# Four edge buffers become six in the message passing of a graph network, and 124 edge groups become 122

## The reference

```
h = relu(layernorm(x));  L0: weighted means over edges, half of the features src->dst, half dst->src
h = relu(layernorm(x));  L1: graph convolution (segment sum of h[src] over dst), then top-2 of 64
                         expert MLPs (256-512-256, gelu) for each node, then batch norm
h = relu(layernorm(x));  L2 ("agnn"), 4 layers:
    logit = beta * cos(h[src], h[dst]);  m = segment_max(logit, dst)
    ex = exp(logit - m[dst]);            h = relu(segment_sum(ex * h[src]) / segment_sum(ex))
h = relu(layernorm(x));  L3 ("gat"), 3 layers, 4 heads of 64, self loops for nodes below 1250:
    h = x @ W;  e = leaky_relu(s_src[src] + s_dst[dst]);  softmax over the edges of a dst
    out = segment_sum(alpha * h[src], dst) + b
```

## Time and profile before

| | us |
|---|---|
| median of 3 runs | 9924.49 (9922.85 to 9927.99) |
| the profiled execution | 9927.93 |
| its span, first to last instruction | 9926.2 |

### The profile page before, as it was taken

The page is one execution under the profiler, slowest core; times in us unless marked ns, Lnnn a source line. Parts: engine busy times, 40 slices in busy tenths (PEclk is TensorE's granted clock), DMA queues, the critical chain, the costliest instruction groups (busy, mean ns, idle before and its releaser), DMA issues. The chain is left out here.

```text
span 9926.2 us, 160244 instructions
## 1 busy us (share of the span) xinstructions
PE 7005.6 (71%) x34788; PEld 5407.3 (54%) x34789; DVE 5926.7 (60%) x21625; ACT 2633.9 (27%) x6946; POOL 5383.8 (54%) x5578
## 2 busy tenths in 40 slices
PE   0003545535663982996996996996799989998997
PEld 0003445534442872885885885885466556655664
DVE  6003334442213225887887887887687768777777
ACT  0001100000000221222222222222455555555554
POOL 0675777747731112775775775774355445534553
PEclk9997557767775996998998998998677677776776
DMA  1301114453440991445445445444333323333333
GB/s 76 137 2 43 48 42 101 101 68 105 105 52 23 345 315 52 100 99 83 100 98 83 100 99 83 100 99 62 74 78 77 66 76 78 78 59 84 77 77 64
DMA packets 621385, 896.33 MB, mean 90 GB/s; under 512 B 289911, under 2 KB 427383, under 8 KB 620062
## 3 DMA queue, kind: packets, MB, share of 16 engines
q0 software_dynamic: 244928, 618.96, 28.9%
q1 hardware_dynamic: 376414, 276.94, 9.2%
HBM read 767.30 MB, written 135.40 MB: 91 GB/s over the span
## 5 line engine op out<-in xcount | busy, mean ns | idle before, releaser
L1510 POOL DMA_INDIRECT hs<-tab_agnn,rec x1984 | 1964.8, 990 | 1114.8 <-issue 593.9
L1944 POOL DMA_INDIRECT hs<-tab_gat,rec x1488 | 1406.4, 945 | 1282.6 <-DVE msg L2013 868.1
L2120 PE MATMUL psV<-msg,ohf 128*128 128x260 f32 x2976 | 1270.9, 603 | 0.8 <-DVE msg L2013 0.8
L1982 DVE CUSTOM_DVE_ANT_0 cand<-psL,neg 128x512 f32<-128x512 f32 x1488 | 991.5, 685 | 265.4 <-issue 176.4
L1531 DVE CUSTOM_DVE_ANT_0 prod<-psG,hs 128x256 f32<-128x256 f32 x1984 | 842.3, 480 | 421.1 <-DMA hs<-tab_agnn,rec 342.8
L2120 PEld LDWEIGHTS psV<-msg,ohf 128*128 128x128 f32 x2976 | 901.0, 317 | 204.1 <-issue 1.2
L1660 PE MATMUL psV<-hs,pr 128*128 128x258 f32 x3968 | 986.1, 392 | 6.2 <-DVE pr L1570 6.2
L1636 PE MATMUL psG<-HN,ohT 128*128 x3968 | 955.6, 384 | 5.1 <-ACT neg L1605 5.1
L626 PE MATMUL psT<-ident,oh 128*128 128x128 f32 x496 | 126.7, 405 | 1023.6 <-DVE oh L592 1023.6
L1636 PEld LDWEIGHTS psG<-HN,ohT 128*128 128x128 f32 x3968 | 725.6, 193 | 86.7 <-issue 6.1
L1660 PEld LDWEIGHTS psV<-hs,pr 128*128 128x128 f32 x3968 | 715.8, 190 | 89.5 <-DVE acc L1557 7.8
(11 more groups left out here) (326 smaller groups left out, 13438.2 us busy)
## 6 DMA issues: line engine op xcount, KB each, us to landing
w<-in_L_gnn_w SPq DMA_DIRECT2D x224, 512.0 KB, 6.0
fwd_d<-acc SPq DMA_DIRECT2D x10, 3224.0 KB, 44.2
fw<-fwd_d SPq DMA_DIRECT2D x124, 260.0 KB
hs<-tab_agnn,rec POOLq DMA_INDIRECT x1984
hs<-tab_gat,rec POOLq DMA_INDIRECT x1488
rec<-rec_d SPq DMA_DIRECT2D x1240, 8.0 KB, 1.7
b<-in_L_gnn_b SPq DMA_DIRECT2D x113, 128.0 KB, 6.4
x<-xbuf SPq DMA_DIRECT2D x112, 128.0 KB, 6.0
```

The lines of the kernel that those rows point to most:

```text
L1510: nc.gpsimd.indirect_dma_start(out=hs[:, j, g, :], out_offset=None, in_=k.tab_agnn, in_offset=bass.IndirectOffsetOnAxis(ap=rec[:, j, g, 0: ...
L1944: nc.gpsimd.indirect_dma_start(out=hs[:, j, g, :], out_offset=None, in_=k.tab_gat, in_offset=bass.IndirectOffsetOnAxis(ap=rec[:, j, g, 0:1 ...
L1982: V.tensor_tensor_reduce(cand[:, m, :], psL[:, m, :], neg[:, h2, :], 1.0, -BIG, ALU.add, ALU.max, mt[:, h2, m:m + 1]).then_inc(s_lt, 1)
L2120: mm = nc.tensor.matmul(psV[:, h4, 0:W_GAT], ohf[:, h4, g, :], msg[:, h4, g, :], start=(g == 0), stop=(g == G - 1))
```

## The change

The ring `U` is 6 in all nine passes, so `rec`, `hs`, `oh` and others get six slots, and a gather of group t waits for group t - 6. The experts keep a ring of 4 under the name `UE`. `NG` is no longer rounded up, so there are 122 groups; since 122 is not a multiple of 6, `pipeline` writes the last two groups out behind the loop, before the drain. The loop runs 19 times instead of 30, and its body is half as long again. Counts of semaphores by slot (`use`, `uses`) follow. In the scatter, fake edges get a place beyond the end of `rec_d`, and the DMA drops what is out of bounds (`bounds_check`). `rec_d` and `fwd_d` have 62,464 rows instead of 63,488.

```diff
@@ -25,10 +25,8 @@
-U = 4
+U = 6
 NG = (E + NB * (GE - 1)) // GE
-NG += -NG % U
-NI = NG // U
...
-MT += -MT % U
+UE = 4
+MT += -MT % UE
...
+def uses(j):
+
+    return NG // U + (j < NG % U)
...
-def pipeline(eng, step, drain, total=NG, numbers=None):
-
-
+def pipeline(eng, step, drain, total=NG, numbers=None, ring=U):
+
+
+    whole = total // ring
     if numbers:
         numbers.load(0)
-    for j in range(U):
+    for j in range(ring):
         step(0, j)
-    with eng.Fori(1, total // U) as i:
+    with eng.Fori(1, whole) as i:
         if numbers:
             numbers.load(i)
-        for j in range(U):
+        for j in range(ring):
             step(i, j)
-    if numbers and drain:
-        numbers.load(total // U)
-    for j in range(drain):
-        step(total // U, j)
+    for n in range(total % ring + drain):
+        if numbers and n % ring == 0:
+            numbers.load(whole + n // ring)
+        step(whole + n // ring, n % ring)
...
-                c.done(nc.vector.scalar_tensor_tensor(out=pos[:, 1, :], in0=mask[:, NB, 1, :], scalar=float(SPARE),
-                                                      in1=pos[:, 1, :], op0=ALU.mult, op1=ALU.add))
-                c.mark(nc.vector.tensor_copy(R[:, :, 4], pos[:, 0, :]))
-                c.mark(nc.vector.tensor_scalar(R[:, :, 3], pos[:, 1, :], float(SPARE), None, ALU.min))
+                c.done(nc.vector.scalar_tensor_tensor(out=pos[:, :, :], in0=mask[:, NB, :, :], scalar=float(SPARE),
+                                                      in1=pos[:, :, :], op0=ALU.mult, op1=ALU.add))
+                for n, col in ((0, 4), (1, 3)):
+                    c.mark(nc.vector.tensor_scalar(R[:, :, col], pos[:, n, :], float(SPARE), None, ALU.min))
...
                                 out=k.rec_rows, out_offset=bass.IndirectOffsetOnAxis(ap=slot[:, n, g, 4:5], axis=0),
-                                in_=slot[:, n, g, 0:4], in_offset=None).then_inc(s_sent[n], 16)
+                                in_=slot[:, n, g, 0:4], in_offset=None, bounds_check=SPARE - 1,
+                                oob_is_err=False).then_inc(s_sent[n], 16)
...
-        use = lambda i: turn * NI + i
+        use = lambda i, j: turn * uses(j) + i
```

More of the change, by code:

```diff
@@ L107, in pick, with lagged @@
     return tile[(slice(None), ds(i, 1)) + rest]
-def lagged(i, j, lag, total=NG):
+def uses(j):
+    return NG // U + (j < NG % U)
+def lagged(i, j, lag, total=NG, ring=U):
     j2 = j - lag
@@ L114, in lagged @@
     while j2 < 0:
-        i2, j2 = i2 - 1, j2 + U
-    t = i2 * U + j2
+        i2, j2 = i2 - 1, j2 + ring
+    t = i2 * ring + j2
     if isinstance(t, int) and not 0 <= t < total:
@@ L142, with __init__ @@
 class Numbers:
-    def __init__(self, nc, eng, table, name, top=NB - 1):
-        self.eng, self.table, self.top = eng, table, top
-        self.regs = [eng.alloc_register(tagged(nc, f"{name}{n}_")) for n in range(2 * U)]
+    def __init__(self, nc, eng, table, name, top=NB - 1, ring=U):
+        self.eng, self.table, self.top, self.ring = eng, table, top, ring
+        self.regs = [eng.alloc_register(tagged(nc, f"{name}{n}_")) for n in range(2 * ring)]
     def load(self, i):
-        self.eng.load(self.regs, self.table[:, ds(i * U, 2 * U)])
+        self.eng.load(self.regs, self.table[:, ds(i * self.ring, 2 * self.ring)])
     def at(self, j, lag):
-        return self.eng.snap(self.regs[U + j - lag], min_val=0, max_val=self.top)
+        return self.eng.snap(self.regs[self.ring + j - lag], min_val=0, max_val=self.top)
     def free(self):
@@ L467, in step @@
                     if not (isinstance(i, int) and i == 0):
-                        sp.wait_ge(q.gather[j], use(i) * (16 * G))
+                        sp.wait_ge(q.gather[j], use(i, j) * (16 * G))
                         sp.sem_inc(q.gate_sp, 1)
@@ L520, in step @@
                         pe.wait_ge(q.u, nth(t - 1))
-                    pe.wait_ge(q.gather[j], use(i) * (16 * G) + 16 * G)
+                    pe.wait_ge(q.gather[j], use(i, j) * (16 * G) + 16 * G)
                     for g in range(G):
@@ L557, in step @@
                     t = i * U + j
[L558 to L562, removed]
+                    if not (isinstance(i, int) and i == 0):
+                        sp.wait_ge(s_sent[j], i * (16 * G))
+                        sp.sem_inc(s_gate_sp, 1)
+                    sp.dma_start(rec[:, j, :, :], k.rec_d[:, ds(t * G, G), :]).then_inc(s_rec[j], 16)
                 pipeline(sp, step, 0)
@@ L1158, in experts @@
         s_b1c = sem("s_b1c")
-        s_x = [sem(f"s_x{n}") for n in range(U)]
-        s_w = [sem(f"s_w{n}") for n in range(U)]
+        s_x = [sem(f"s_x{n}") for n in range(UE)]
+        s_w = [sem(f"s_w{n}") for n in range(UE)]
         s_bias = sem("s_bias")
@@ L1167, in experts @@
         s_ys = sem("s_ys")
-        s_out = [sem(f"s_out{n}") for n in range(U)]
+        s_out = [sem(f"s_out{n}") for n in range(UE)]
         s_gate = sem("s_gate")
@@ L1217, in step @@
                 def step(i, n):
-                    t = i * U + n
+                    t = i * UE + n
                     pool.wait_ge(s_ys, t + 1)
@@ L1221, in step @@
                     pool.dma_start(k.ybuf_t[ds(t, 1), :, :].rearrange("a p c -> (a p) c"), y[:, n, :]).then_inc(s_out[n], 16)
-                pipeline(pool, step, 0, MT)
-                for n in range(U):
-                    pool.wait_ge(s_out[n], MT // U * 16)
+                pipeline(pool, step, 0, MT, ring=UE)
+                for n in range(UE):
+                    pool.wait_ge(s_out[n], MT // UE * 16)
             @block.vector
@@ L1250, in step @@
                         nc.vector.tensor_tensor(y[:, m, :], psy[:, m % 2, 0:D], b2[:, m, :], ALU.add).then_inc(s_ys, 1)
-                pipeline(dve, step, 2, MT, numbers=tiles)
+                pipeline(dve, step, 2, MT, tiles, UE)
             @block.scalar
@@ L1255, in step @@
                 def step(i, n):
-                    if last := lagged(i, n, 1, MT):
+                    if last := lagged(i, n, 1, MT, UE):
                         _, m, t = last
@@ L1265, in step @@
                         g.then_inc(s_g, 1)
-                pipeline(act, step, 1, MT)
+                pipeline(act, step, 1, MT, ring=UE)
             @block.tensor
@@ L1276, in step @@
                 def step(i, n):
-                    if now := lagged(i, n, 0, MT):
+                    if now := lagged(i, n, 0, MT, UE):
                         i0, m, t = now
@@ L1303, in step @@
                         mm.then_inc(s_y, 1)
-                pipeline(pe, step, 2, MT)
+                pipeline(pe, step, 2, MT, ring=UE)
 def combine(nc, k, a):
@@ L1485, in attention_by_angle @@
                 nth = lambda t: layer * NG + (2 * NG + t)
-                use = lambda i: layer * NI + (2 * NI + i)
+                use = lambda i, j: layer * uses(j) + (2 * uses(j) + i)
                 own = flow = lambda t: layer * NG + t
```

68 lines of the change are left out of this document (34 added, 34 removed).

## The result

| | us |
|---|---|
| kernel before | 9923.67 (9918.89 to 9927.99, 4 runs) |
| changed kernel | 9754.11 (9748.81 to 9756.55, 4 runs) |
| ratio, 95% interval | 0.9829 (0.9812 to 0.9846) |
| profiled execution of the change, its span | 9754.8, 9753.1 |

The change is faster by 170 us, or 1.7%. The forecast was 9656, a gain of 269; the time lies in the range of 9510 to 9790, near its slow end.

The account below looks back on a forecast made before the run. POOL, PE and DVE lie close in agnn's groups with edges, DMA bounds those without, PE bounds gat; -133 - 80 - 35 - 28 + 2 + 5 = -269 from 9927.9, less 3.4, gives 9656 (range 9511 to 9790).

Parts of the forecast that it names:

- loads of twelve numbers: Block-number loads in gat's loop: twelve instead of eight cost 0 to 0.30 us more each, 0 to 18 us, taken as 4.
- Two groups fewer: Every pass loses two groups without edges, at the price of its tail: 133 us saved together, called the surest term.
- No ring helps there: agnn's groups without edges: all gathers read one table row, DMA bounds them at 6.67 us; only fewer groups help.
- still at some 6.7 us: Sign for the profile after: agnn's groups without edges keep this pace, queue over 90% busy, but 11 of them.
- The ring in agnn: agnn's groups with edges: POOL's waits should vanish, pace from 5.43 to 5.25 us a group, 80 us saved (0 to 155).
- under 5 us a pass: Sign for the profile after: POOL's wait for PE's sums in agnn's groups with edges, before 28.6 us a pass.
- The ring in gat: gat's groups with edges: PE's 11.8 us a pass of waits for gathers go, 35 us saved (0 to twice that).
- rival 2: gat wins more, as six slots remove many slow groups: 133 us gained there instead of 63, time 9586; chance 0.13.
- fewer branches: gat's loop: 11 fewer branches a pass at 0.98 us, 32 us over three passes, net 28 after longer loads.
- Longer code: agnn's branches back between passes might start to pay a stall, 0 to 10 us, taken as 5; inner loops no refetch.
- rival 3: gat's loop no longer fits the code DVE holds; branches back cost up to 3.40 us each, at most +194, 9850; chance 0.07.
- Rivals 1 and 4: 1: POOL falls into step with DVE, ring wins nothing, 9798, chance 0.14; 4: gat's clock falls, slower, 10,025, chance 0.06.

Follow-up runs that it names:

- ring of 4: The changed kernel with a ring of 4 instead of 6, still 122 groups: 9800.40 us, 0.9876 of the kernel before; on a slower chip 0.9912.
- aligned: The changed kernel with each iteration's twelve block numbers stored apart, at multiples of 48 bytes: 9579.01 us, 0.9647 of the kernel before; on a slower chip 10,945.72, 0.9939.
- the body of 407: DVE's gat loop with a ring of 8 instead of 6, on the aligned kernel with pads spread over the table: 9624.95 us, 0.9697 of the kernel before.
- its repeat: The changed kernel run once more, unaltered, beside the second ring-of-4 run: 9758.71 us, 0.9829 of the kernel before.

## Why the prediction was right or wrong

The sign and the range held; the sum was 97 us too good. Two errors are behind that, and they go against each other: the loads of twelve numbers cost 176 us more than forecast, and the ring with short loads won 74 more. That the time fell within the range is in part luck.

| term | predicted | measured |
|---|---|---|
| two groups, scatter, outer code | -133 + 2 + 5 = -126 | -131 (ring of 4 against before) |
| ring and branches, loads of 12 aligned | -80 - 35 - 32 = -147 | -221 (aligned against ring of 4) |
| loads of 12 against 8 | +4 | +180 (change against aligned) |
| sum | -269 | -172 |

Where the time went shows by PE's sums, from the profiled executions: from the first group of a pass to its 111th, the last with edges, and from there to the last group, in us over the four passes of agnn and the three of gat.

| | before | ring of 4, 122 groups | change | aligned |
|---|---|---|---|---|
| agnn, to the 111th group | 2410 | 2397 | 2383 | 2300 |
| agnn, behind it | 330 | 287 | 254 | 257 |
| gat, to the 111th group | 2352 | 2340 | 2354 | 2253 |
| gat, behind it | 275 | 229 | 210 | 206 |

So the change won 27 us in agnn's groups with edges, where 80 were forecast, and lost 2 in gat's, where 63 were; the tails gave 141 instead of 97. The rows for agnn's first pass, of the ring of 4 and then of the aligned kernel, in each the sums of the first, the 111th and the last group:

```profile
3913.30 1.99 PE L1665 MATMUL psV<-hs,pr 128*128 128x258 f32 x8
4512.65 1.99 PE L1665 MATMUL psV<-hs,pr 128*128 128x258 f32 x8
4582.54 2.01 PE L1665 MATMUL psV<-hs,pr 128*128 128x258 f32 x8 [1.47 <-DVE pr L1575]
...
3934.40 1.99 PE L1670 MATMUL psV<-hs,pr 128*128 128x258 f32 x8
4509.07 1.99 PE L1670 MATMUL psV<-hs,pr 128*128 128x258 f32 x8
4572.60 2.01 PE L1670 MATMUL psV<-hs,pr 128*128 128x258 f32 x8 [1.47 <-DVE pr L1580]
```

*Two groups fewer.* Right in size; the 131 hold the longer outer code and the scatter, too.

*"No ring helps there."* This step of the prediction failed, to the change's good. From the ring of 4 to the aligned ring of 6 the groups without edges took 30 us less in agnn and 23 in gat, though the queue was still 93% busy. The sign that I gave for it, "still at some 6.7 us", failed with it: it was 5.6.

*The loads of twelve numbers.* This is the step that cost the most: "Twelve cost between nothing more and 0.30 more, so 0 to 18 us in all; I take 4." I scaled the duration of the earlier trace rows by the count and didn't ask where each load begins. All 256 loads in those rows began at a multiple of 16 bytes, so the trace of before could not show the other kind; the stride of 24 bytes was to be read from the code, and I should have named it as an operation that the trace doesn't show. A long load comes 10 times a pass. It costs an agnn iteration about 2.1 us (33.45 against 31.36) and a gat iteration 3.4. 4 x 10 x 2.1 + 3 x 10 x 3.4 = 186, near the 180 measured. In the table it is 83 and 101 in the groups with edges.

*The ring in agnn.* The forecast fits once the loads are short: POOL's waits went from 28.6 to 2.1 us, and the pace by PE's iterations is 5.23 where I took 5.25, "PE at 5.08 plus its share of the loop's branch". From the ring of 4 that is 97 us in the groups with edges, for the 80. That the greater depth did it isn't shown. In the change itself the long loads of DVE held back the sums and hence POOL (a wait of 4.2 us). The profile was to show "5.2 to 5.3 us" and waits "under 5 us a pass"; it showed 5.31 and 20.4, and this mismatch was the first sign of the missing term.

*The ring in gat.* In the change nothing is left of it. With short loads the groups with edges take 99 us less than before, halfway between the 63 of the forecast and the 133 of rival 2, and in kind it is rival 2 that was right: slow stretches went away, more than waits for gathers. Three iterations in a row of the ring of 4, all engines:

```profile
7003.07:7030.46 27.39, 26.84 (x115) 17.90 (x115) 22.62 (x94) 16.78 (x44) 15.10 (x17) 0.75 0.31 81
7030.46:7061.47 31.01, 28.86 (x113) 18.36 (x113) 22.84 (x94) 16.52 (x44) 15.13 (x17) 0.67 0.34 71
7061.47:7088.86 27.39, 26.50 (x117) 17.48 (x116) 22.68 (x94) 16.78 (x44) 15.11 (x17) 0.75 0.32 81
```

Undisturbed it runs at 27.39 / 4 = 6.85 us a group, the same as the 41.0 / 6 = 6.83 of the ring of 6. The difference is the other iterations, which lose up to 3.6 us and, as the one shown, have a lower clock. With six slots and short loads hardly any of them is left: from the third to the last but one, the iterations of the first pass are between 40.9 and 41.0 us. agnn shows the same: its loop takes 20.9 us undisturbed with the ring of 4, so 5.23 a group as with the ring of 6, but many iterations take 22 to 23. Why the disturbed ones are gone, by more slots or by the longer body, is open. The 28 us that I gave to fewer branches can't be seen in the 6.85 against 6.83; what is saved in branches goes into the longer load. That the 9579 without the long loads is close to rival 2's 9586 is a coincidence, since the tails gave 53 of it.

*Longer code.* Two places. The branch back between agnn's passes did begin to pay: from PE's last sum of a pass to DVE's first `oh` of the next the trace has 44.2 us before and 48.1, 48.1 and 47.9 after, 12 us in all, where I had 0 to 10 and took 5. With the ring of 4 it is 47, so most of it seems to come from the two groups written out behind the loop. The inner loops pay nothing at 307 instructions (rival 3 is wrong for this change) and do at 407. The inner loops' sizes, 4 blocks fetched in a pass against 71, agree with the rule of the Trainium skill that I had weighed (Runtime: NRT & Kernel Launch, Instruction fetch mechanics: two pages of 256, and a stop when a branch goes out of them), if the body of 407 touches three pages, which no run here shows.

*Rivals 1 and 4.* POOL did not fall into step with DVE: gathers at 413.76 / 426 = 0.97 us each, against 0.99. gat's clock neither fell nor, in the change, rose.

*What has no step.* The experts' stage, whose code is the same, ran 8 us longer in the profiled execution of the change than in that of before, and 4 longer in that of its repeat. From the ring of 4 to the aligned kernel, too, the stages ahead of agnn took 20 us more, which the -221 of the table above hold. I have no cause for either.

## What to carry to other kernels

When a change alters how much one operation takes at a time, look at where each of them begins and not only at how long it is: the earlier trace rows were right for what they showed and for nothing else. A small load at the head of a loop costs its whole length when it stops an engine that others wait for, and in gat 1.7 times that (3.4 us for 2.0), where the clock was lower behind it. And a deeper ring is to be judged by the spread of its iterations: the gain was not a faster undisturbed iteration but that the disturbed ones went away, up to the size at which the loop's code had to be fetched again. Last, a window that begins while the buffers fill makes a deeper ring look better than it is; the consumer's work, from the first group to the last, doesn't.

## What the runs showed of the hardware

- A load of numbers into registers is short if it begins at a multiple of 16 bytes, and long if it doesn't: 0.59 against 1.85 us for eight, 0.85 against 2.74 for twelve on DVE, 1.94 and 2.89 for the long ones on PE. The steps are those of four numbers at a time against one by one, but for the one aligned load of four, at 0.59.
- Beside DMAs at 422 to 436 GB/s each such access took 0.94 to 1.0 us, where the quiet loads differ by 0.22 to 0.26 an access; sixteen numbers beginning at 4 bytes took 15.1 us.
- Gathers that all read one row of a table are slow: spread over the table they gained 58 us.
- A loop body of 407 DVE instructions had its code fetched again (71 blocks in gat's first pass) and stood 4.4 us at each head; bodies of 307 and 256 did not.
- Two of the chips used ran the kernel before in 11,010 and 11,023 us, the others in 9924 to 9931. On the first of these two the aligned ring of 6 was 48 us slower than the ring of 4, on a quick one 221 faster.
